# Attention with P read one step after it is written and four P buffers, against a lag of three and five steps and six buffers

## The reference

```python
q = (x @ Wq.T).reshape(N, S, H, hd).transpose(0, 2, 1, 3)      # k and v alike
energy = jnp.einsum('nhqd,nhkd->nhqk', q, k)
attn = jax.nn.softmax(energy / jnp.sqrt(jnp.float32(hd)), axis=3)
out = jnp.einsum('nhql,nhld->nhqd', attn, v)
x = _layernorm(x + out)
# router: softmax, top 6 of 16, renormalised gates
for e in range(E):
    out = out + x1 @ expert_w[e] * gate[:, e:e + 1]
x = _layernorm(x1 + out)
```

## Time and profile before

| what | value |
|---|---|
| two runs | 2943.47 and 3027.68 us, median 2985.57 us |
| profiled execution, its own time | 2938.12 us |
| span of its slowest core (core 6) | 2936.6 us |
| spans of the eight cores | 2924.2 to 2936.6 us |
| stage 1, by core 6 | 0 to about 340 us |
| stage 2 (attention) | about 340 to 1600 us |
| stage 3 | about 1600 to 2937 us |
| busy over the span: PE, ACT, DVE | 80%, 38%, 24% |

### The profile page before, as it was taken

How to read it: one execution, slowest core, us unless ns; L and a number is a source line. 1 busy time by engine, 2 the same in 40 slices (tenths; PEclk the granted TensorE clock), 3 DMA queues, 4 the chain that set the end, 5 groups by cost and what they waited for, 6 DMA issues and landing times.

```text
span 2936.6 us, 32035 instructions; the slowest of 8 cores (2924.2 to 2936.6 us)
## 1 busy us (share of the span) xinstructions
PE 2360.8 (80%) x12032; PEld 903.7 (31%) x12032; DVE 718.7 (24%) x1555; ACT 1118.7 (38%) x1153; POOL 59.8 (2%) x80
## 2 busy tenths in 40 slices
PE   6996989888988888888887434899995343899996
PEld 2442322222222222222222111344442111344442
DVE  2332200000000000000001343233336444233336
ACT  0000388888888888888886010000000101000000
POOL 1000100000000000000000000000000000000000
PEclk9998899999999999999998666999998676899998
DMA  6755899940000000000001100222123000222221
GB/s 88 106 72 81 104 112 110 113 51 1 1 1 1 1 1 1 1 1 1 1 1 54 40 22 0 90 83 86 58 86 129 22 15 8 86 86 66 79 86 58
DMA packets 48018, 146.91 MB, mean 50 GB/s; under 512 B 2752, under 2 KB 23264, under 8 KB 46848
## 3 DMA queue, kind: packets, MB, share of 16 engines
q0 software_dynamic: 43264, 128.09, 24.1%
q1 hardware_dynamic: 4608, 16.78, 1.6%
HBM read 197.32 MB, written 41.94 MB: 81 GB/s over the span
## 4 chain that ended last, share of the span: by engine, by line
PE 69%; ACT 12%; DVE 10%; issue 5%; DMA 4%; DVEq 1%; ACTq 0%; POOL 0%; SPq 0%; POOLq 0%
PE s_PS L713 30%; PE s_PS L388 13%; PE s_PS L301 10%; ACT s_RC L446 9%; PE s_PS L225 5%; PE s_PS L288 5%; PE s_PS L246 4%; DVE s_RC L536 2%; DMA s_RC<-xfm 1%; PE s_PS L313 1%; ACT s_RC L443 1%; DMA s_RC<-xqf 1%; DMA s_RB<-ewb 1%; DVE s_RA L727 1%; DVE s_RC L543 1%
## 5 line engine op out<-in xcount | busy, mean ns | idle before, releaser
L713 PE MATMUL s_PS<-s_RB,s_QO 128*128 128x512 bf16 x4096 | 931.5, 391 | 137.7 <-DVE s_gates L669 67.6
L388 PE MATMUL s_PS<-s_QO,s_RA 64*128 64x512 bf16 x2048 | 581.6, 398 | 106.7 <-ACT s_RC L446 76.2
L443 ACT ACTIVATE s_RC<-s_PS,s_cb 128x1024 bf16<-128x1024 f32 x512 | 570.6, 1114 | 182.8 <-PE s_PS L388 177.8
L713 PEld LDWEIGHTS s_PS<-s_RB,s_QO 128*128 128x128 bf16 x4096 | 407.3, 100 | 658.0 <-issue 208.1
L446 ACT ACTIVATE s_RC<-s_PS,s_cb 128x1024 bf16<-128x1024 f32 x512 | 567.3, 1108 | 2.4 <-PE s_PS L388 1.9
L288 PE MATMUL s_PS<-s_RC,s_RB 128*64 128x512 bf16 x2048 | 316.0, 390 | 39.3 <-DVE s_RC L364 25.5
L771 ACT ACTIVATE s_tE<-s_tB 128x1 f32<-128x1 f32 x16 | 3.2, 203 | 881.3 <-DVE s_tB L763 881.3
L301 PE MATMUL s_PS<-s_RC,s_ozb 128*64 128x512 bf16 x2048 | 330.1, 411 | 1.3 <-DVE s_rzpre L326 0.5
L362 DVE CAST s_QO<-s_PS 128x1024 bf16<-128x1024 f32 x16 | 19.6, 1224 | 1148.1 <-PE s_PS L301 1148.1
L388 PEld LDWEIGHTS s_PS<-s_QO,s_RA 64*128 64x128 bf16 x2048 | 116.5, 94 | 528.6 <-issue 527.9
L730 DVE SCALAR_TENSOR_TENSOR s_RB<-s_PS,s_gates,s_RA 128x1024 f32<-128x1024 f32 x128 | 164.2, 1283 | 275.4 <-PE s_PS L713 275.4
(11 more groups left out here) (76 smaller groups left out, 638.2 us busy)
## 6 DMA issues: line engine op xcount, KB each, us to landing
s_RB<-ewb POOLq DMA_DIRECT2D x32, 2048.0 KB, 9.8
ewb<-ew POOLq DMA_DIRECT2D x16, 2048.0 KB, 166.6
s_RC<-xfm POOLq DMA_DIRECT2D x16, 1024.0 KB, 10.2
s_RC<-xtm SPq DMA_DIRECT2D x16, 512.0 KB, 3.5
y<-s_RC SPq DMA_DIRECT2D x16, 512.0 KB, 2.7
s_RC<-xqf POOLq DMA_DIRECT2D x4, 1024.0 KB, 16.3
s_RC<-wkT POOLq DMA_DIRECT2D x1, 2048.0 KB, 17.4
s_QO<-wvT POOLq DMA_DIRECT2D x1, 2048.0 KB, 24.3
```

The lines of the kernel that those rows point to most:

```text
L388: ins = t.matmul(PS[:, head * 1024 + qc * 512: head * 1024 + (qc + 1) * 512], RA[rows, c * SQ + kc * 128: c * SQ + (kc + 1) * 128], QO[row ...
L443: sc.activation(P[:, 0:1024], PS[:, 0:1024], AF.Exp, bias=cb3[:, :], scale=0.125).then_inc(sE, 1)
L713: ins = t.matmul(PS[:, pb + jh * 512: pb + (jh + 1) * 512], QO[:, dc * TOK + t_i * 128: dc * TOK + (t_i + 1) * 128], wbuf(par)[:, dc * 102 ...
```

## The change

- P has four buffers, taken as kc mod 4. ScalarE waits before exp(kc) for Z(kc-4), and only from kc = 4 on.
- A step becomes S(kc), PV(kc-1), Z(kc-3). PV starts at kc = 1 and Z at kc = 3. PV(kc-1) waits for the exp of both heads of kc-1.
- `ftPVt` and `ftZt` at the end of a pass are gone; PV(29) and PV(30) and Z(27) and Z(28) now stand in the steps kc 30 and 31 themselves.
- In the next pass, Z(29), Z(30) and Z(31) follow S(0) and wait for the last exp; PV(31) follows S(1), then come VectorE's two copies (`fve`); the transposes follow S(2).
- PV(0) therefore stands behind S(1) and PV(31), and Z(0) behind S(3) and PV(2). Their waits for VectorE are as before.
- `zs` and the small tiles of stage 3 move to other columns of `RC`.

```diff
-    def emit_pv(t, c, kcp, first, last, p_idx=0):
-        P = pbuf((32 * p_idx + kcp) % 6)
+    def emit_pv(t, c, kcp, first, last):
+        P = pbuf(kcp % 4)
...
         def ftZl(t, cc=cc, exp_need=pvl_exp_need[p_prev]):
+            t.wait_ge(sE, exp_need)
             for kcp in (NKT - 3, NKT - 2, NKT - 1):
...
                 if p > 0:
-                    if kc == 1:
-                        emit_pvl(p - 1)
+                    if kc == 0:
+                        emit_zl(p - 1)
+                    elif kc == 1:
+                        emit_pvl_fve(p - 1)
                     elif kc == 2:
-                        emit_zl(p - 1)
-                    elif kc == 4:
                         emit_ftz(p - 1)
-                if kc >= 5:
-                    kcz = kc - 5
...
-                if kc >= 3:
-                    kcp = kc - 3
+                if kc > 0:
+                    kcp = kc - 1
                     ve_need = fve_cnt.get(p - 1, 0) if kcp == 0 else 0
-                    def ftPV(t, c=c, kcp=kcp, exp_need=max(0, exp_need - 4),
-                             ve_need=ve_need, p=p):
+                    def ftPV(t, c=c, kcp=kcp, exp_need=exp_need, ve_need=ve_need):
                         t.wait_ge(sE, exp_need)
                         if ve_need > 0:
                             t.wait_ge(vE, ve_need)
...
+                zl = []
+                if kc >= 3:
+                    zl = [kc - 3]
...
-                        pv_need=(z_cnt.get((p, kc - 6), 0) if kc >= 6
-                                 else z_cnt.get((p - 1, kc + 26), 0))):
+                def fse(sc, s_done=s_done, kc=kc,
+                        pv_need=(z_cnt.get((p, kc - 4), 0) if kc >= 4 else 0)):
...
-            for kcp in (NKT - 3, NKT - 2):
-                def ftPVt(t, c=c, kcp=kcp, exp_need=csE.v, p=p):
-                    t.wait_ge(sE, exp_need)
...
-            for kcz in (NKT - 5, NKT - 4):
-                def ftZt(t, c=c, kcz=kcz, p=p):
```

More of the change, by code:

```diff
@@ L103, in pbuf @@
         return RC[:, par * 2048:(par + 1) * 2048]
-    zs = RC[:, 12288:14336].bitcast(dt.float32)
+    zs = RC[:, 8192:10240].bitcast(dt.float32)
     def x0stage(par):
@@ L111, in build @@
     usq_f32 = RC[:, 6144:8192].bitcast(dt.float32)
[L112 to L118, removed]
+    x1b = RC[:, 12288:13312]
+    e16 = RC[:, 13312:13344].bitcast(dt.float32)
+    lgt = RC[:, 13344:13376].bitcast(dt.float32)
+    mx8 = RC[:, 13376:13392].bitcast(dt.float32)
+    sel = RC[:, 13392:13424].bitcast(dt.float32)
+    t16 = RC[:, 13424:13456].bitcast(dt.float32)
+    t16b = RC[:, 13456:13488].bitcast(dt.float32)
     def ot32(par):
@@ L294, in emit_pv, with emit_z @@
         return ins
-    def emit_z(t, c, kcp, first, last, p_idx=0):
-        P = pbuf((32 * p_idx + kcp) % 6)
+    def emit_z(t, c, kcp, first, last):
+        P = pbuf(kcp % 4)
         for head in range(2):
@@ L334, in build, with ftZl @@
     pvl_exp_need = {}
-    def emit_pvl(p_prev):
-        cc = p_prev % NPAIR
-        def ftPVl(t, cc=cc, exp_need=pvl_exp_need[p_prev]):
-            t.wait_ge(sE, exp_need)
[L341 to L344, removed]
     def emit_zl(p_prev):
         cc = p_prev % NPAIR
-        def ftZl(t, cc=cc, p_prev=p_prev):
+        def ftZl(t, cc=cc, exp_need=pvl_exp_need[p_prev]):
+            t.wait_ge(sE, exp_need)
             for kcp in (NKT - 3, NKT - 2, NKT - 1):
-                ins = emit_z(t, cc, kcp, False, kcp == NKT - 1, p_prev)
+                ins = emit_z(t, cc, kcp, False, kcp == NKT - 1)
             ins.then_inc(tV, 1)
@@ L356, in emit_zl, with emit_pvl_fve, ftPVl @@
             z_cnt[(p_prev, kcp)] = ctV.v
+    def emit_pvl_fve(p_prev):
+        cc = p_prev % NPAIR
+        def ftPVl(t, cc=cc, exp_need=pvl_exp_need[p_prev]):
+            t.wait_ge(sE, exp_need)
+            emit_pv(t, cc, NKT - 1, False, True).then_inc(tV, 1)
+        q("tensor", ftPVl)
+        ctV.v += 1
+        pv_cnt[(p_prev, NKT - 1)] = ctV.v
         pvz_done = ctV.v
@@ L430, in ftPV @@
                             t.wait_ge(vE, ve_need)
-                        emit_pv(t, c, kcp, kcp == 0, False, p).then_inc(tV, 1)
+                        emit_pv(t, c, kcp, kcp == 0, False).then_inc(tV, 1)
                     q("tensor", ftPV)
@@ L434, in build, with ftZ @@
                     pv_cnt[(p, kcp)] = ctV.v
-                def fse(sc, s_done=s_done, kc=kc, p=p,
-                        pv_need=(z_cnt.get((p, kc - 6), 0) if kc >= 6
-                                 else z_cnt.get((p - 1, kc + 26), 0))):
+                zl = []
+                if kc >= 3:
+                    zl = [kc - 3]
+                if zl:
+                    ve_need = fvz_cnt.get(p - 1, 0) if zl[0] == 0 else 0
+                    def ftZ(t, c=c, zl=tuple(zl), ve_need=ve_need):
+                        if ve_need > 0:
+                            t.wait_ge(vE, ve_need)
+                        for kcp in zl:
+                            ins = emit_z(t, c, kcp, kcp == 0, False)
+                        ins.then_inc(tV, 1)
+                    q("tensor", ftZ)
+                    ctV.v += 1
+                    for kcp in zl:
+                        z_cnt[(p, kcp)] = ctV.v
+                def fse(sc, s_done=s_done, kc=kc,
+                        pv_need=(z_cnt.get((p, kc - 4), 0) if kc >= 4 else 0)):
                     if pv_need > 0:
                         sc.wait_ge(tV, pv_need)
-                    P = pbuf((32 * p + kc) % 6)
+                    P = pbuf(kc % 4)
                     sc.wait_ge(tS, s_done - 1)
@@ L449, in build @@
                 csE.v += 2
-            for kcp in (NKT - 3, NKT - 2):
-                def ftPVt(t, c=c, kcp=kcp, exp_need=csE.v, p=p):
[L453 to L457, removed]
-            for kcz in (NKT - 5, NKT - 4):
-                def ftZt(t, c=c, kcz=kcz, p=p):
[L460 to L463, removed]
             pvl_exp_need[p] = csE.v
-    emit_pvl(2 * NPAIR - 1)
     emit_zl(2 * NPAIR - 1)
+    emit_pvl_fve(2 * NPAIR - 1)
     emit_ftz(2 * NPAIR - 1)
```

## The result

The changed kernel is faster by 1.3%, which is clear of none: the ratio of its runs to those of the kernel before is 0.9868, 95% interval 0.9854 to 0.9882. The profiled execution took 2900.2 us (before 2938.1), the span of its slowest core, now core 3, 2898.7 (before 2936.6). The forecast was 2904 us, 34 less than the profiled execution of before; measured are 38.

The account below looks back on a forecast made before the run. TensorE's queue was taken to set the end, holding 69% of the chain of waits. Changes of pass falling from 102 to 69 us, plus the tail's 1.7, take 2938.1 to 2904 us; range 2889 to 2919, with rivals 2868 to 2948.

Parts of the forecast that it names:

- The middle of a pass: Steady loop of attention: S, PV, Z sums to 1.50 us as before, two steps stay 4.46; nothing taken, bounds 7 us.
- the rival that PV's wait costs in every loop: Steady loop: PV's new wait costs although met, 240 times; at 0.45 us each the kernel takes 3012 us; chance 0.08.
- The change of pass at full clock: Between passes of attention: exp(5) comes 15.85 us after exp(31), an excess of 2.4 us against 3.7 before.
- The tail as the source of the gain: Change of pass: with the tail removed, S(0) starts at 1.30 us after exp(31) instead of 4.11.
- The clock: TensorE's clock falls at 14 of 15 changes of pass, costing 2.35 us each (1.8 to 2.9), against 3.3 before.
- the prediction's own sign: Changes of pass: prediction is wrong if falls number far from 14 or one costs anything but 1.8 to 2.9 us.
- low from the end of the stall until about 14.5: Change of pass: half clock from the stall's end at 8.0 us until about 14.5 puts exp(4) 1.8 us late.
- The sum: All changes of pass cost 69 us against 102, a gain of 33; with the tail's 1.7, 34 to 35.
- The 1.4 us gained in the first pass was put at 0: First pass of attention: PV and Z start two steps earlier, partly at half clock; taken as 0, bounds 2 us.
- what follows attention: Stage 3 has the same instructions and only other columns of SBUF; taken as 0.
- The rule of the Trainium skill: Clock falls need a longer unbroken idle gap than either queue has, so none would come; kept as a rival.
- The tail at the very end: Behind the very last exp of attention: four groups fewer at 0.43 us each, a gain of 1.7 us.

Follow-up runs that it names:

- e6: The kernel before, with only PV(kc-3) queued ahead of Z(kc-5) in each step; ratio 0.9997 to the kernel before.
- e4: The changed kernel with six P buffers instead of four and ScalarE waiting for Z(kc-6); ratio 0.9872 to the kernel before.
- e1: The kernel before, with only PV(29), PV(30), Z(27), Z(28) moved behind S(0) of the next pass; ratio 0.9843 to the kernel before, 2896.3 us.
- e5: e3 with the eight transposes queued behind PV(1), not ahead of it; ratio 0.9693 to the kernel before, 2852.8 us.
- e2: The kernel before, with VectorE's copy of the PV sum right behind PV(31) and PV(0) waiting for it alone; ratio 0.9913, 2912.7 us.
- e3: The changed kernel with PV(31) and its copy behind S(0), Z(29 to 31) behind S(1), PV(0) awaiting that copy alone, six buffers; ratio 0.9749 to before.
- e8: e5 with Z(kc-3) queued between the S of head 0 and of head 1, from kc = 4 on; ratio 0.9781 to the kernel before.

## Why the prediction was right, and where it was off

- *The middle of a pass* was to stay as it was. It did: in the changed kernel the exps of head 0 still start 2.01 and 2.46 us apart in turn, together 4.47 as before, by which the rival that PV's wait costs in every loop has fallen. Two more parts were tried one by one, the order by e6 (0.9997) and the buffers by e4 (0.9872 against 0.9868).
- *The change of pass at full clock* was to take 15.85 us from exp(31) to exp(5). It takes 15.88. The laid-out queue was also right inside: PV(0) 8.0 us after exp(31), measured 499.95 - 491.92 = 8.03; exp(2) at 9.27, measured 9.29; VectorE's wait 2.5 to 2.7, measured 2.62.
- *The tail as the source of the gain* was argued in the prediction and is shown by e1, whose 15.60 us is also the value worked out for it. The prediction did not say that the remaining edits may cost something. They do, 0.0025 to 0.0029 or 7 to 9 us. About 4 of them are 15 times the 0.28 us between 15.88 and 15.60, whose likely place is PV(0)'s wait, 2.62 us against 2.02: in e1 S(3) stands between the group whose end starts VectorE's copies and PV(0), in the changed kernel nothing does. The clock has a part too: falls of 6.8 us come 0 to 2 times per core in e1, 3 or 4 times in the changed kernel.
- *The clock* is the term that was mis-sized. The count was right (15 falls on three cores, 14 on five; 14 forecast). The price of one was to be 2.35 us, from 1.8 to 2.9. By the distance from exp(31) to exp(5), 17.3 to 17.6 us against 15.88, it is about 1.5 us where the clock was low for 3.4 us, as in 11 of 15 on core 3, and 2.6 (18.5 us) in three of the four with 6.8; the fourth, the first change of pass, takes 19.2 us. By the length of a pass, 75.6 and 76.6 to 76.9 us against 74.36 in the one pass of core 6 without a fall, it is 1.2 and 2.3 to 2.6. Either way the price in most changes lies below 1.8, so by the prediction's own sign this term was wrong. The step that failed is "low from the end of the stall until about 14.5": the clock did fall about then, 7.2 to 9.4 us after exp(31), but mostly it came back after 3.4 us and not after 6.5. This is a fall in core 3, exp(31) to exp(5) in 17.44 us:

```profile
947.82 1.11 ACT L447 ACTIVATE s_RC<-s_PS,s_cb 128x1024 bf16<-128x1024 f32 x1 [0.34 <-PE s_PS L389]
...
955.85 0.88 PE L288 MATMUL s_PS<-s_RC,s_RB 128*64 128x512 bf16 x4 [2.62 <-DVE s_RC L365]
...
959.53 0.63 PE L288 MATMUL s_PS<-s_RC,s_RB 128*64 128x512 bf16 x4
...
965.26 1.11 ACT L447 ACTIVATE s_RC<-s_PS,s_cb 128x1024 bf16<-128x1024 f32 x1 [0.34 <-PE s_PS L389]
```

  The PV after the stall, at 955.85, is already part slow (0.88), and the one at 959.53 fast again (0.63).
- *The sum.* Taken together, the steps beyond the steady pace come to 1211.3 - 511 x 2.236 = 68.7 us, against 1248.0 - 1142.6 = 105.4 before. Of these 2.3 and 3.7 lie in the first pass, so the changes of pass went from 102 to 66, where the prediction had 102 and 69. The 1.4 us gained in the first pass was put at 0, within bounds of 2. That the total came within 4 us is in part luck: it is the difference of two cores' spans, in which stage 1 lost 2.4 and what follows attention gained 1.9. The prediction had nothing for the one and 0 for the other.
- *The rule of the Trainium skill* ("TensorE: Matmul & The Clock Gate", section "HAM oscillation — how this bites in real kernels"), by which no gap here is long enough for a fall, disagrees with the new trace too: on core 3 the clock falls 15 times, at 14 gaps of 2.6 us and one of 3.0. In e5 it fell 8 times on eight cores with no gap over 0.5 us at the changes of pass.
- *The tail at the very end* gave 1.7 us, as worked out.

What stays open is what decides whether the clock falls at a change of pass. The falls, counted over the cores of the profiled executions, are these:

| PV(0)'s wait for VectorE | tail ahead of S(0) | falls, of so many changes of pass |
|---|---|---|
| 1.65 to 2.0 us | yes (before) | 110 of 120 |
| 2.0 us | no (e1) | 108 of 120 |
| 2.6 us | no (the changed kernel) | 115 of 120 |
| none | yes (e2) | 47 of 120 |
| none | no (e3, cores 4 to 7) | 7 of 60 |
| none | no (e5) | 8 of 120 |

So the wait has the larger part in how often the clock falls, and the tail a part once the wait is gone; that the idle time of TensorE links the two is argued and not shown. The old falls began ahead of the wait of their own change of pass, and these edits also move everything else in time, by which the falls may differ as well.

## What to carry to other kernels

When two engines hand work to each other in a loop, queue nothing that has to wait between the last piece of one pass and the first of the next: here four matmul groups, the first of which waited for the last exp, kept the next S, and so ScalarE, back by 2.7 us at each of 15 changes. Then look at what the next stall is: here two copies in a row behind one semaphore, of which the waiting matmul needed the first alone. Laying the instruction queue out piece by piece, with start-to-start times from the trace, gave both to within 0.1 us; the clock has to be priced apart, and its price was the least certain term.

## What the runs showed of the hardware

- The granted clock can stay at 0.50 with TensorE busy without a break: in e8, on 6 of 8 cores, for the whole first pass of 121 us, with matmuls of half the rows and half the columns in turn and a change between them four times a step. On core 5, the same program left 0.50 about 12 us into the first pass and then ran at 1.00. With the order S, S, PV, Z it rose 11 to 13 us after the first exp on all eight cores (e5, first pass 74.0 to 74.1 us). So the order decides whether a core can be caught here; what in it holds the clock down, and what set the two free cores apart, is not shown.
- The four S matmuls of a step take 0.54 us together when both heads are free (1528.61 to 1529.15), and two take 0.51 when one head has to wait and goes alone (1003.63 to 1004.14).
- The four pieces of a step with a change between row and column tiles at each take 2.18 us, and the old start-to-start times, 0.51 ahead of a column tile and 0.56 ahead of a row tile, had given 2.14. So the changes could be priced from rows of the old trace.
